# A two-layer graph network in fp32: the second layer's rows kept in SBUF, and wider broadcasts of target numbers in the first aggregation

## What is computed

```python
xn = layernorm(x)
x  = x + gat_and_mlp(xn, edges) + mixer0(xn)          # first layer: softmax over edges, linear attention
x  = x + moe0(layernorm(x))                           # two of 8 experts, chosen once for the whole graph
xn = layernorm(x)
x  = x + gnn1(xn, edges, edge_weight) + mix1(xn)      # second layer
x  = x + moe1(layernorm(x))                           # two of 8 experts per node

def gnn1(xn, ...):      # weighted sum of the source rows of each target, after a 256x256 matrix
    return relu(segment_sum((xn @ weight)[src] * edge_weight[:, None], dst))

def mix1(fx, ...):      # 8 heads of 32
    x_mid = layernorm1(fx) @ Wx.T + bx
    q = softmax(x_mid @ Wq.T, axis=-1)                # over the 32 of a head
    k = softmax(x_mid @ Wk.T, axis=-2)                # over the nodes
    h = (q @ (k.T @ v)) @ Wo.T + bo + fx
    return gelu(layernorm2(h) @ W1.T + b1) @ W2.T + b2 + h
```

## Time and profile before

| what | value |
|---|---|
| median of 3 runs | 2543.21 us (2519.75 to 2543.67) |
| profiled execution, its own time | 2550.95 us |
| its span | 2549.3 us |
| instructions in the span | 32299 |
| granted TensorE clock, mean | 0.775 of full |

### The profile page before, as it was taken

The page is one execution under the profiler, slowest core; times in us unless marked ns, Lnnn a source line. Parts: engine busy times, 40 slices in busy tenths (PEclk is TensorE's granted clock), DMA queues, the critical chain, the costliest instruction groups (busy, mean ns, idle before and its releaser), DMA issues. The chain is left out here.

```text
span 2549.3 us, 32299 instructions
## 1 busy us (share of the span) xinstructions
PE 1697.1 (67%) x8125; PEld 1324.4 (52%) x8125; DVE 1348.8 (53%) x4006; ACT 668.5 (26%) x2205; POOL 1138.2 (45%) x1279
## 2 busy tenths in 40 slices
PE   4635565566666596989954677766767777665493
PEld 3533344344444485888843355544545555444492
DVE  4724576666679586566652544433434444355334
ACT  1213233243244232466631010000000010111251
POOL 2754676677640022222223555544545555224441
PEclk8765777777678898999976877877877788756696
DMA  4742344444430553555522222222223233113586
GB/s 149 211 138 80 108 113 111 111 118 117 113 84 1 170 172 100 190 181 171 169 92 85 80 85 83 85 81 83 85 81 89 85 92 92 52 40 110 158 265 215
DMA packets 199721, 296.17 MB, mean 116 GB/s; under 512 B 31657, under 2 KB 153683, under 8 KB 199308
## 3 DMA queue, kind: packets, MB, share of 16 engines
q0 software_dynamic: 52704, 143.00, 19.7%
q1 hardware_dynamic: 100470, 104.99, 13.3%
q10 hardware_dynamic: 46390, 46.37, 5.4%
HBM read 215.21 MB, written 80.13 MB: 116 GB/s over the span
## 5 line engine op out<-in xcount | busy, mean ns | idle before, releaser
L452 POOL DMA_INDIRECT ring<-feat_d,src_lane x440 | 440.1, 1000 | 255.2 <-issue 117.8
L1085 POOL DMA_INDIRECT rows<-xn_d,src_lane x440 | 423.6, 963 | 188.0 <-issue 127.2
L1075 PE MATMUL bank<-ring,a_hot 128*128 128x260 f32 x880 | 327.4, 526 | 194.8 <-DVE acc L965 65.6
L1158 PE MATMUL bank<-rows,a_hot 128*128 128x256 f32 x880 | 283.7, 437 | 134.9 <-issue 78.0
L1139 DVE TENSOR_TENSOR acc<-bank,acc 128x256 f32 x440 | 186.5, 424 | 346.0 <-DMA ring<-in_x 260.8
L1075 PEld LDWEIGHTS bank<-ring,a_hot 128*128 128x128 f32 x880 | 213.9, 260 | 270.9 <-issue 127.0
L1158 PEld LDWEIGHTS bank<-rows,a_hot 128*128 128x128 f32 x880 | 172.4, 214 | 216.0 <-issue 197.9
L965 DVE TENSOR_TENSOR acc<-bank,acc 128x260 f32 x440 | 186.4, 424 | 121.5 <-DMA xnT_d<-ring 45.3
L1011 ACT ACTIVATE ring<-ring 128x64 f32<-128x64 f32 x880 | 215.9, 334 | 15.3 <-issue 14.3
L1998 PE MATMUL bank<-x_lnT,x_w 128*128 128x128 f32 x800 | 121.2, 306 | 97.1 <-ACT x_lnT L1954 53.5
L1998 PEld LDWEIGHTS bank<-x_lnT,x_w 128*128 128x128 f32 x800 | 114.6, 219 | 104.8 <-ACT x_lnT L1954 56.3
(11 more groups left out here) (386 smaller groups left out, 3160.8 us busy)
## 6 DMA issues: line engine op xcount, KB each, us to landing
slots_d<-e_blank ACTq DMA_DIRECT2D x25, 1300.0 KB, 5.6
e_w_now<-in_L_ffn_w SPq DMA_DIRECT2D x56, 256.0 KB
a_dst_bc<-dst_lo_d SPq DMA_DIRECT2D x47, 256.0 KB
big<-in_L_ffn_W SPq DMA_DIRECT2D x16, 512.0 KB
e_x<-slots_d SPq DMA_DIRECT2D x56, 130.0 KB
ring<-feat_d,src_lane POOLq DMA_INDIRECT x440
rows<-xn_d,src_lane POOLq DMA_INDIRECT x440
e_ys<-y_d SPq DMA_DIRECT2D x24, 256.0 KB
```

The source lines that it names most:

```text
L452: pool.indirect_dma_start(ring[:, q % RING, at, :], None, table, bass.IndirectOffsetOnAxis(ap=src_lane[:, n:n + 1], axis=0)).then_inc(gath ...
L1075: pe.matmul(bank[at][:, 0:D + H], hot[:, q % HOTS, at, :], ring[:, q % RING, at, :], start=True, stop=True)\
L1085: pool.indirect_dma_start(rows[:, n % RING1, :], None, table, bass.IndirectOffsetOnAxis(ap=src_lane[:, n:n + 1], axis=0)).then_inc(gathere ...
L1158: pe.matmul(bank[s % 4][:, 0:D], hot[:, n % HOTS, :], rows[:, n % RING1, :], start=True, stop=True)\
```

## The change

1. First aggregation: 24 broadcast loads of 16 steps (512 KB, the last 8 steps) into two buffers of two chunks, in place of 47 of 8 steps (256 KB) into three. Each is asked for when all but three compares before its first chunk are done.
2. First experts: x2 is written into `acc` (row width 260, of which 256), xn2 into a tensor of all 25 tiles in SBUF, q^T over the first layer's transposed rows in SBUF. The stores of x2 and q^T are gone; xn2's stays, since the gathers read it. DVE takes the maximum of k per tile (`top_k`). All lists are written out.
3. Second mixer: the maximum comes from the 25 maxima per half, the exponential goes in five parts per half, ahead of PE; no cuts, PE turns k where it lies. b2 is added to all rows of x2, bo to `folded` (each head's q sums to 1, so a row of bo added to one head's 32 rows is bo).
4. Second aggregation: sums go into the room of k (`agg`), cleared by POOL before its first gather. The mixer's MLP reads q^T, xn2 and x2 from SBUF and leaves its sum in `acc`; SP only loads five weights at the start, W1 and W2 into v's room. The two products with a row of ones are gone.
5. Second graph stage: no loads of the mixer's part and no cuts; PE turns `agg` where it lies. The loads of the second experts' first weights follow at once on SP.

The core of the diff:

```diff
 # first_aggregate
-            for u in range(UP_FIRST, NS // UP):
-                v = u - UP_FIRST
-                once(sp, hot_ready, v - L + 1)
-                sp.dma_start(dst_bc[:, v % L, :],
+            for u in range(UP_FIRST, NS // UP, 2):
+                w, n = (u - UP_FIRST) // 2, min(2, NS // UP - u)
+                once(sp, hot_ready, 2 * w - 2)
+                sp.dma_start(dst_bc[:, w % 2, 0:n, :],
 # first_experts
-                pool.dma_start(rows_of(x2_d, g), x2[:, j, :]).then_inc(x2_stored[j], 16)
-                act.dma_start(qT_d[bass.ds(g, 1), :, :].rearrange("a p n -> p (a n)"), qT[:, j, :])\
-                   .then_inc(qT_stored[j], 16)
+                act.activation(xn1T[:, :, g * P:(g + 1) * P], q_ps[:, 0:D].rearrange("p (k n) -> p k n", k=KT), ACT.Copy)\
+                   .then_inc(qT_ready, 1)
+            def top_k(i, j):
+                g = i * R + j
+                dve.wait_ge(k_ready, g + 1)
+                known = min(NP, N_NODES) - g * P if g == T - 1 else P
+                dve.tensor_reduce(tops[:, :, g], big_k[:, :].rearrange("p (k n) -> p k n", k=KT)[:, :, g * P:g * P + known],
+                                  AX, ALU.max)
-            pipeline(dve, [(4, norm_again), (5, divide), (3, norm_x), (2, residual), (4, cut), (1, add_y)])
+            pipeline(dve, [(4, norm_again), (5, divide), (3, norm_x), (2, residual), (4, cut), (5, top_k), (1, add_y)], **whole)
 # second_mixer
-            link(dve.memset(k_view[:, :, N_NODES:NP], 0.0))
-            link(dve.tensor_reduce(peak[:, :], k_view[:, :, 0:N_NODES], AX, ALU.max))
+            link(dve.tensor_reduce(peak[:, :], tops[:, :, :], AX, ALU.max))
+            dve.tensor_scalar(peak[:, :], peak[:, :], -1.0, None, ALU.mult).then_inc(peak_ready, 1)
+            link(dve.memset(k_view[:, :, N_NODES:NP], 0.0))
+            dve.wait_ge(b2_in, 16)
+            link(dve.tensor_tensor(x2[:, :, 0:D], x2[:, :, 0:D], b2[:, :].unsqueeze(1).broadcast_to([P, T, D]), ALU.add))
+            dve.wait_ge(exp_ready, KT * NI)
+            link(dve.tensor_reduce(total[:, :], part_total[:, :, :], AX, ALU.add))
             link(dve.reciprocal(total[:, :], total[:, :]))
-            def cut_tile(i, j):
+            link(dve.tensor_tensor(folded[0:SM, 0, :], folded[0:SM, 0, :], bo[:, :], ALU.add))
+                for k in range(KT):
+                    last = pe.transpose(bank[g % 2][:, k * P:(k + 1) * P], k_view[:, k, g * P:(g + 1) * P], ident)
 # second_aggregate
+            pool.memset(agg[:, :, :], 0.0).then_inc(zeroed, 1)
             pipeline(pool, [(0, gather)] + extra["gpsimd"](pool), **unrolled)
-            dve.memset(acc[:, :, :], 0.0).then_inc(zeroed, 1)
-            dve.wait_ge(zeroed, 1)
+                if n == 0:
+                    dve.wait_ge(zeroed, 1)
 # mixer_mlp
-                sp.dma_start(x_in[:, :], rows_of(x2_d, g)).then_inc(loaded, 16)
-                sp.dma_start(xn_in[:, :], rows_of(xn2_d, g)).then_inc(loaded, 16)
-                sp.dma_start(qT_in[:, :], qT_d[bass.ds(g, 1), :, :].rearrange("a p n -> p (a n)")).then_inc(loaded, 16)
-                sp.dma_start(rows_of(mixed_d, g), mixed[:, :]).then_inc(stored, 16)
-                pe.matmul(h_ps, ones, vec[:, 0, :], start=True, stop=False)
+                    last = pe.matmul(h_ps, qT[:, k, g * P:(g + 1) * P], folded[:, k, :],
+                                     start=(k == 0), stop=(k == KT - 1))
-                    pe.matmul(y_ps[:, 0:D], ones, vec[:, 1, :], start=True, stop=False)
 # second_graph
-                sp.dma_start(mixed[:, j, :], rows_of(mixed_d, g)).then_inc(loaded[j], 16)
-                dve.tensor_copy(sums[:, j, :], tile_of(acc, g)[:, 0:D]).then_inc(sums_ready, 1)
-                    last = pe.transpose(s_ps[g % 2][:, k * P:(k + 1) * P], sums[:, j, k * P:(k + 1) * P], ident)
+                    last = pe.transpose(s_ps[g % 2][:, k * P:(k + 1) * P], agg[:, g, k * P:(k + 1) * P], ident)
```

More of the change, by code:

```diff
@@ L262, in program @@
[L262 to L272, removed]
+            xn2, tops = sb("xn2", [P, T, D], ctx=kept), sb("k_tops", [P, KT, T], ctx=kept)
@@ new lines, in program @@
+            folded = sb("folded", [P, KT, D], ctx=kept)
+            agg = big_k.rearrange("p (t n) -> p t n", t=T)
+            with Stage(nc) as held:
+                rows = sb("rows", [P, RING1, D], ctx=held)
+                gathered = [held.semaphore(f"rows_gathered{r}") for r in range(RING1)]
+                second_mixer(nc, A, hold, bank, const, big_k, big_v, tops, folded, acc, src_lane, xn2_d, rows, gathered)
+                second_aggregate(nc, bank, const, agg, step_tile, src_lane, dst_lane, ew_lane, xn2_d, rows, gathered,
+                                 mixer_mlp(nc, A, hold, bank, const, folded, xnT, xn2, acc, big_v))
@@ L1101, in _ @@
         def _(sp):
-            extra["before"]["sync"](sp)
-            pipeline(sp, extra["sync"](sp), **unrolled)
-            extra["after"]["sync"](sp)
+            extra["sync"](sp)
         @block.gpsimd
@@ L1544, in load @@
                 sp.dma_start(xn1_in[:, j, :], rows_of(xn1_d, g)).then_inc(loaded[j], 16)
-            pipeline(sp, [(0, load)])
-            for j in range(R):
-                for s in (x2_stored, xn2_stored, qT_stored):
-                    sp.wait_ge(s[j], 16 * NI)
+            pipeline(sp, [(0, load)], **whole)
+            sp.wait_ge(xn2_stored, 16 * T)
         @block.gpsimd
@@ L1822, in copy_ek @@
+            act.wait_ge(peak_ready, 1)
+            exponents(0)
+            for g in range(T):
+                if g % R == 0 and g // R + 1 < NI:
+                    exponents(g // R + 1)
                 act.wait_ge(turned, g + 1)
                 once(act, summed, g - R + 1)
-                act.activation(ek[:, j, :], bank[j % 2][:, 0:D], ACT.Copy).then_inc(ek_ready, 1)
-            pipeline(act, [(0, copy_ek)])
+                act.activation(ek[:, g % R, :], bank[g % 2][:, 0:D], ACT.Copy).then_inc(ek_ready, 1)
@@ L1828, in _, with add @@
         @block.tensor
         def _(pe):
-            pe.wait_ge(w_in, 16)
+            def add(g):
+                pe.wait_ge(ek_ready, g + 1)
+                for m in range(KT):
+                    last = pe.matmul(bank[4 + m][:, 0:P], ek[:, g % R, m * P:(m + 1) * P], big_v[:, g, m * P:(m + 1) * P],
+                                     start=False, stop=False)
+                last.then_inc(summed, 1)
             for m in range(KT):
                 pe.matmul(bank[4 + m][:, 0:P], zero, ident, start=True, stop=False)
-            def turn(i, j):
-                g = i * R + j
-                pe.wait_ge(cut, g + 1)
-                once(pe, ek_ready, g - bank_gap(j) + 1)
+            pe.wait_ge(step, 2)
@@ L2017, in beside @@
         return dict(
-            before=dict(sync=before), after=dict(sync=after),
-            sync=lambda sp: [at(0, FRONT, load(sp)), at(1, BACK, store(sp))],
+            sync=load,
             gpsimd=lambda pool: [at(2, BACK, lambda g: norm.root(pool, g))],
```

208 lines of the change are left out of this document (86 added, 122 removed).

## The result

The changed kernel takes 2457.14 us (median of 4, 2447.98 to 2459.89), the kernel before 2541.57 on the same chip: a ratio of 0.968 (95% interval 0.9621 to 0.9739), 84 us less. The forecast was 54 less; the measured time lies in its range of 2430 to 2532. The profiled executions differ by more, 2550.95 and 2456.04, since the profiled execution of before took 9 us more than its median.

What follows compares the result with a forecast made beforehand. No engine is full throughout; in the second aggregation, PE's work must fit around standstills in POOL's gathers. Terms 0 - 3 - 7 + 0 - 37 - 2 - 5 = -54 give 2489 us by the median, range 2430 to 2532.

Steps and rivals of the forecast that it cites:

- TensorE's work in a turn is on the path: Second aggregation's 25 turns of 16 steps: removing the ones-row products L1976 (25.3 us) and L2007 (23.4) gives -37.
- rival B: Second aggregation: long turns of 34.67 us also fall to the short kind, 31 us more, 2458 in all; chance 0.17.
- seven late copies: Second aggregation: ACT's copy of turned, normed h (L1954) held until the standstill's end 7 times, 4.5 us each.
- The standstill: In long rows of POOL's gathers, almost nothing but POOL moves for some 12 us; forecast to remain.
- rival C: Second aggregation: the standstill goes, being made by SP's loads; 280 us, 2246 (softer form 2386); chance 0.06 for both.
- it goes with the row of gathers, whatever makes it: The standstill also occurs in gather rows without the mixer's MLP beside them, 1415 to 1431 and 1343.5 to 1368.5.
- Graph stage: Second graph stage: mixed's loads and DVE's 25 cut copies go, the copy being on the tile's cycle; -5, range -12 to +2.
- (D): Second aggregation: less PE work keeps the clock at half level, short turns become long; +81 against -54, 2570; chance 0.07.
- Second mixer: PE starts ten us earlier, some 8 more tiles fit before the standstill, b2's addition on DVE; -7, range -11 to +1.
- Start of the second aggregation: DVE's memset of the sums goes, POOL clears instead in up to 7.8 us; 0, range -5 to +3.
- Experts: First experts: stores go, DVE's maximum of k mostly hidden, end about 2.5 us shorter; -3, range -10 to +5.
- The rule on branches: First experts: taken branches break instruction prefetch, so unrolling might win up to 5.5 us more; not counted in the sum.

Runs made afterwards that it cites:

- its second: The changed kernel itself, unedited, run again on another chip with standstills: 2479.86 us, 0.9609 of the kernel before.
- the second pair of traces: The changed kernel and the kernel before, both unedited, profiled again on another chip with standstills: 2479.86 and 2576.45 us.
- the memsets: Changed kernel plus a POOL memset of 256 numbers per partition after each gather of the second aggregation: 2244.79 us, 1.0555 of the kernel before.

## Why the prediction was right, and where it was off

*Direction and bound.* The step that carried the forecast held, that TensorE's work in a turn is on the path though TensorE is 71% busy: putting 49 us of it back cost 41 us against the changed kernel's first trace (26 against its second, from a slower chip). The term was -37, L1976 in full and L2007 by half, so it was sized well; both in full would have been -49. Per turn, those with a timely copy went from 30.25 us on average before (30.28 with the products back) to 28.57, 1.7 us for 1.97 us of PE's work (in the second pair of traces 30.37 to 29.10, 1.3 us).

*The long turns (rival B).* The time came out at rival B's 2458, and that is in part luck. B wanted 70 us from the second aggregation (37, 31 and 2) and got 57.6; the rest came from the graph stage, 17 us more than forecast. B's mechanism is half borne out. Taking the products out does bring every copy ahead of the standstill, and putting them back makes eight late again. But a late copy doesn't make a long turn by itself; how late it is goes with the turn's length, as the 120 turns of the five traces with standstills show:

| copy after its root, us | turn, us | copies |
|---|---|---|
| 6.3 to 10.7 | 26.0 to 32.0 | 97 |
| 13.4 to 17.6 | 28.5 to 30.8 | 8 |
| 18.3 to 19.7 | 30.5 to 32.6 | 7 |
| 21.8 to 23.5 | 34.7 to 35.9 | 8 |

The forecast priced seven late copies at 4.5 us each, 31 us. Its own trace had 24 distances of which three were near 34.7, which is 13 us over the short kind; the second trace of before has five. The trace with the products back has none past 19.7 us, and its eight late turns are 30.05 us on average, no longer than its others. So the turns' part of the stage's 57.6 us is 39 us for the products and 14 us for the long turns (24 times the differences of the means, 30.77, 30.20 and 28.57), and 5 us come at the stage's ends. What kept the copies with the products back from coming as late as 21.8 us is among the rest of the stage's changes (SP's loads and their waits, where the rows lie), or the chip; this is open.

*The standstill.* It stayed where the forecast said, so rival C (it goes away with SP's loads) is out. But "it goes with the row of gathers, whatever makes it" was half true. In three of the six groups of runs some 400 gathers came almost in one row at the same pace, 1.26 us, and nothing stood still. It takes a row of gathers and a chip that has it. All that the forecast says of turns holds for such a chip only; on the others the whole change is worth under 1%, by the kernels that carried all of it and one addition (the changed kernel itself was not run there).

*Graph stage, the term that was mis-sized.* -5, with a range of -12 to +2; measured -21.7 (-20.1 in the second pair of traces). "The copy is on the tile's cycle" was right and worth 0.3 us: where a tile ran at the low clock without the copy it took 4.66 us, with it 4.97 or 4.90. What was missed is that PE's clock is part of the cycle. The 24 distances between tiles add up to 136.8 us before and 115.2 in after, and that is the 21.7. In after 13 of them are 3.36 or 3.37 us, at a granted clock of 0.93 to 1.00; before, none is under 3.87, and 18 of the 24 are at 0.50 or 0.51. In after a tile at full clock holds 1.9 us of PE's work, and one at the lower clock 3.5 us. The groups of the largest product say the same, 44.9 us for 100 matmul records before, with a mean of 599 ns, and in after:

```profile
L2208 PE MATMUL bank<-g_w,g_sumsT 128*128 128x256 f32 x100 | 36.1, 498 | 0.0
```

A rival on the clock was in the forecast (D), but for the slower side and for the aggregation, where it did not occur: the good stretch of after's turn has 0.98. Why one copy of 0.28 us goes with the lower clock is not shown by any run, only that it does.

*Second mixer.* -7 forecast, -5.5 measured. PE's first transpose came 2.4 us after the start, earlier than foretold, and the standstill stayed at about 17 us after the first gather. But the addition of b2 was not free, as the timeline of the stage's start shows:

```profile
1317.12 0.20 DVE L1790 TENSOR_REDUCE m_peak<-k_tops 128x2 f32<-128x50 f32 x1 [1.98 <-PEq L85]
...
1319.44 1.09 PE L1845 MATMUL bank<-const,big 128*128 128x128 f32 x4 [1.12 <-ACT big L1817]
1320.46 6.83 DVE L1794 TENSOR_TENSOR acc<-acc,m_b 128x6400 f32<-128x6400 f32 x1 [2.78 <-DMA m_b<-in_L_mix_b]
1321.65 6.47 POOL L1087 DMA_INDIRECT rows<-xn_d,src_lane  x1 [0.30 <-issue]
```

The gather at 1321.65 takes 6.47 us and not 0.96: it ends 0.8 us after DVE's addition does. POOL's row of 32 gets 5.5 us longer by it (45.6 us from first to last, 40.3 before), and the standstill lasts as long as the row. I had laid the addition on DVE alone. What the stage would take without it was not run.

*Start of the second aggregation.* 0 forecast; the first addition came 6.99 us after the stage's start, 7.35 before. Right by a sum of two errors: POOL's clear took 5.43 us and not 7.8, but DVE stood for as long:

```profile
1381.44 5.43 POOL L1116 MEMSET big<- 128x6400 f32 x1 [18.05 <-POOLq L85]
1381.48 6.30 DVE L1126 TENSOR_SCALAR a_hot<-const,dst_lane,ew_lane 128x128 f32<-128x128 f32 x5 [1.01 <-PEq L85]
```

Five matrices of edge weights take 6.30 us here and 1.37 in the kernel before. Moving the clear from DVE to POOL took nothing off DVE here.

*The small terms.* Broadcasts: 0, and the stage differs by -2.2 and +7.4 us in the two pairs of traces. The second lies outside the term's range of -2 to +4, but the compare never waited (22.5 us in 47, idle 0.0 before it, in the first trace), and the run with the products back, with the same first aggregation, took 626.6: no loss is shown. Experts: -3 against -4.3 and -1.6; PE's only idle time before L1713 is again 5.5 us at the entry, so the straight code won nothing there, as the row had said. The rule on branches that the forecast took from the Trainium skill (Runtime: NRT & Kernel Launch, Instruction fetch mechanics) has a condition that the forecast left out: it speaks of a taken branch whose target lies outside the current window of two pages. No run here shows such a stall.

## What to carry to other kernels

A turn that is cut by a standstill is priced by all that an engine has to do between two of them, even if that engine is idle a third of the time; put such work back alone to see how much of a gain it was. Before a gain is told as a kernel's, the kernel before must be timed on the same chip, and on more than one: this one takes 2130 us on some and 2540 to 2580 on others, and the change is worth 3 to 4% there and under 1% here. In a short cycle of TensorE and VectorE, count what the cycle costs at both clock levels: with a copy of 0.28 us in it the stage kept mostly to the lower one, without it six or more of 24 tiles ran at the higher one. And look before a long DVE instruction is laid beside POOL's work, or a long POOL instruction beside DVE's: an addition with two inputs in SBUF held a gather up until it had ended, a reduction of about the same length did not.

## What the runs showed of the hardware that was not expected

- *Chips of two kinds.* Six groups of runs on at least five chips: in three of them the kernel before took 2128 to 2130 us, in the other three 2542 to 2576. In the changed kernel and its variants the difference is in stretches with gathers: second mixer 50 against 64, second aggregation 546 to 555 (679 with the memsets) against 753 to 795, first aggregation 522 to 527 against 627 to 635, first mixer 42 against 67 to 69, while the experts take 298 to 302. A gather takes 0.96 us on either, the DMA packets of its rows 0.16 us in the median on either, and instructions are fetched as often and as fast (in the second aggregation 43 to 45 packets of instructions, the larger kind 1.0 to 1.2 us in the median). What makes TensorE nearly stop there is not known; the Trainium skill (SBUF — State Buffer, Who interferes with whom) says that PE and ACT never wait on anyone at SBUF's ports, so by it the cause is elsewhere; no run here tells.
- *VectorE and GpSimd hold each other up for whole instructions.* A memset of 5.43 us on POOL stretched a tensor_scalar of DVE to 5.47 us (0.34 else), and a two-input addition of 6.83 us on DVE a gather of POOL to 6.47 (0.96 else). Both stand in all twelve traces that have these pairs (the gather 6.45 to 6.80) and in neither of before. Not every long instruction does it: before, DVE's reduction of 6.67 us ran beside five gathers of 0.96 to 1.04 us. The Trainium skill (SBUF — State Buffer, Who interferes with whom) has both: a DVE instruction in a two-port mode, or one with two SBUF inputs against a GpSimd instruction that reads SBUF, takes a pair of ports for its whole length, and whichever comes first blocks the other. Both cases agree with the trace: tensor_scalar is among the ops for which it names such a mode, and the gather reads its list of rows from SBUF.
- *The clock of a short cycle.* The graph stage ran at a mean clock of 0.52 to 0.56 and took 178.6 to 183.0 us in all three traces with the copy; without it, in eleven, it took 158.7 to 169.4, at 0.58 to 0.70. Within one stage without the copy single tiles take either 3.36 us, at 0.89 to 1.00, or 4.66, at 0.50; in after the low ones follow tiles of 9.1 to 9.3 us in which PE is busy for 4.0.
